# VectorE's path sums split around the sum of paths, the causal mask moved behind them

## The chip, the cores and the metric

One core of one Trainium2 chip runs the whole kernel. The metric is device time in microseconds (us) of one execution. Five engines work side by side, each in the order of its own program and tied to the others by semaphores: PE (TensorE, matmuls; its weight loads are listed as PEld), DVE (VectorE), ACT (ScalarE), POOL (GpSimd) and SP (SyncE, which here only issues DMAs).

## The reference

A decoder block over 32 sequences of 128 tokens, width 256, all in fp32:

```
x = layernorm(x + attn(x));  x = layernorm(x + cross_attention(ctx, x));  x = layernorm(x + moe(x))

attn: q, k, v = silu(conv4(x @ Wq | Wk | Wv));  beta = sigmoid(x @ Wb)
      delta = delta rule in chunks of 32 (a triangular inverse and a running state)
      paths = [fir3(v), fir15(v), fir64(v), delta, v]                 # 5 paths, 4 heads of 64
      stats = (mean, mean square, mean |.|, norm) of each path and head
      probs = softmax(gelu([x, stats] @ gW1 + gb1) @ gW2 + gb2, scaled) with a floor
      o = sum_p probs_p * paths_p;   out = (o * rsqrt(mean(o*o))) @ Wo
```

The change lies in the second half of attn: the solution of the delta rule, the statistics, the gate, the weighted sum of the paths, the output product and the first layernorm.

## The kernel before

The program runs stages one after the other: constants, projections, inverses and filters, `mix_paths`, then cross-attention, routing, experts and the final sum. Only `mix_paths` is touched. It handles the 32 sequences as 16 pairs. Every engine runs `staged_pair_loop(engine, 16, (step, lag), ...)`: in turn n each step of the list is done, in the order written, for pair n - lag. Several pairs are so in flight at once, and the written order of each list is the order in which that engine does its work. The semaphores say what a step must wait for; a step that waits holds up all that stands behind it on the same engine. Below, turn n is named after this count, and a turn is measured from one start of `shift_logits` on DVE (line L1104) to the next.

The lists are these, with the lag in brackets.

- DVE before: delta_sums (2), square_sums (2), mask_scores (1), sum_paths (3), mix_norm (3), path_sums (1), scale_mix (3), scale_delta (1), residual (3), shift_logits (2), ln_shift (3), probabilities (2).
- PE: scores (1), cross_blocks (1), then solve_rows(0) to (3) (1) alternating with hidden_x(0) to (3) (2), delta_rows (1), statsT (2), mixedT (3), hidden_stats (2), output (3), logits (2).
- ACT: square_delta (2), keep_cross (1), keep_rows(0) to (2) (1), square_mix (3), keep_rows(3) (1), square_paths (1), copy_stats (2), copy_mixed (3), gelu twice (2), exps (2), normalize (3).
- POOL: weight (3), norms (2), make_rhs (0), mix_inverse (3), ln_inverse (3).

The steps that matter here, with their lines: `mask_scores` (L1060) multiplies the scores of `scores` (L842), in PSUM, by the causal mask; `delta_rows` (L886) on PE multiplies the masked scores with the solution rows, and waits for `masked` and for the last `keep_rows` (L983). `path_sums` (L1083 on the three filtered paths, L1084 on the value) sums each path and its magnitude over each head, for both sequences t = 0 and 1 of the pair, eight reductions in all. `sum_paths` (L1140, L1145, L1148) adds the weighted paths and waits for POOL's `weight` (L1231). `mix_norm` (L1154, L1157) needs ACT's square (L1028); POOL's `mix_inverse` (L1239) takes the power -1/2; `scale_mix` (L1163) applies it; `mixedT` (L940) transposes the result for `output` (L948). `statsT` (L893) transposes the statistics of the pair before, `copy_stats` (L1001) moves them to SBUF, `hidden_stats` (L918) is the gate's first product with them, `gelu` (L1012), `logits` (L928), `shift_logits` and `probabilities` follow.

Of the kernel before, what the change touches and what calls it, by code (L numbers as in the profile page):

```python
# [75 lines left out]
def staged_pair_loop(eng, count, *stages):  # L76


    most = max(lag for _, lag in stages)
    fill = most + most % 2 + 2  # L80

    def turn(n):
        for step, lag in stages:
            if 0 <= n - lag < count:
                step((n - lag) // 2, (n - lag) % 2)

    for n in range(fill):
        turn(n)
    with eng.Fori(fill // 2, count // 2) as j:
        for u in range(2):  # L90
            for step, lag in stages:
                step(j + (u - lag) // 2, (u - lag) % 2)
    for n in range(count, count + most):
        turn(n)
# [28 lines left out]
def is_early(j, u, count):  # L123

    return isinstance(j, int) and 2 * j + u < count
# [25 lines left out]
def value_heads(M, n):  # L151

    return M.value[:, :, bass.ds(n, 1), :].rearrange("p (h k) b c -> p h k (b c)", k=HK)
# [7 lines left out]
def filtered_heads(M, n):  # L161

    return M.filtered[:, :, :, bass.ds(n, 1), :].rearrange("p f (h k) b c -> p (f h) k (b c)", k=HK)
# [536 lines left out]
def mix_paths(nc, M):  # L700
# [7 lines left out]
    P, W, PW = 2, DV * H, 2 * DV * H  # L708
    PAIRS = B // P
    with signals(nc) as signal, ExitStack() as ctx:  # L710
# [53 lines left out]
        statsT_mm = signal("statsT_mm")  # L764
# [32 lines left out]
        def tile(j, u, t):  # L797
            return P * (2 * j + u) + t
# [252 lines left out]
        def _(dve):  # L1051
# [20 lines left out]
                                  wide(M.rq[:, pairs(j, u), :].rearrange("p b h -> p (b h)"), [128, P * H, DV], 2),  # L1072
                                  ALU.mult).then_inc(delta_kept, 1)

            def path_sums(j, u):
                i = 2 * j + u
                if not is_early(j, u, 2):

                    dve.wait_ge(statsT_mm, i - 1)
                for t in range(P):  # L1080
                    fir, val = filtered_heads(M, tile(j, u, t)), value_heads(M, tile(j, u, t))
                    for s, mag in ((0, False), (2, True)):
                        dve.tensor_reduce(stat[:, u, t, 0:12, s], fir, AX.XY, ALU.add, apply_absolute_value=mag)  # L1083
                        dve.tensor_reduce(stat[:, u, t, 16:20, s], val, AX.XY, ALU.add, apply_absolute_value=mag)  # L1084

            def delta_sums(j, u):
                i = 2 * j + u
                dve.wait_ge(delta_kept, i + 1)
                for s, mag in ((0, False), (2, True)):
                    dve.tensor_reduce(stat[:, u, :, 12:16, s], delta[:, u, :, :].rearrange("p b (h d) -> p b h d", d=DV),  # L1090
                                      AX.X, ALU.add, apply_absolute_value=mag)
# [92 lines left out]
            def ln_shift(j, u):  # L1184
# [4 lines left out]
                dve.scalar_tensor_tensor(out=ln_s[:, :], in0=mv[:, :, 0], scalar=-1.0, in1=ln_r[:, :], op0=ALU.mult,  # L1189
                                         op1=ALU.mult).then_inc(shift_made, 1)  # L1190

            staged_pair_loop(dve, PAIRS, (delta_sums, 2), (square_sums, 2), (mask_scores, 1), (sum_paths, 3), (mix_norm, 3),
                             (path_sums, 1), (scale_mix, 3), (scale_delta, 1), (residual, 3), (shift_logits, 2), (ln_shift, 3),
                             (probabilities, 2))

        @block.gpsimd
        def _(pool):
# [1125 lines left out]
```

## Time and profile before

| | |
|---|---|
| time, three runs | median 2091.64 us (2087.59 to 2106.17) |
| the profiled execution | 2096.82 us, its span 2095.1 us |
| busy over the span | PE 1568.9 us (75%), PEld 1231.9 (59%), DVE 1011.6 (48%), ACT 634.0 (30%), POOL 647.8 (31%) |
| mean granted TensorE clock | 0.794 of full |

Times in the rows are us from the start of the span. The granted clock is a share of 2.4 GHz, so 1.00 is 2.4 GHz and 0.50 is 1.2 GHz. The mixing stage is one fifth to one quarter of the span, so what the change does there has to be read from this stage, not from the shares of the table.

### The profile page before, as it was taken

What the parts mean: (1) busy time and instruction counts of PE and PEld (TensorE: products, weight loads), DVE (VectorE), ACT (ScalarE), POOL (GpSimd) and SP (SyncE); (2) the same over time, 40 slices, a digit from 0 to 9 for tenths busy, and PEclk for the clock granted to TensorE, in tenths of its full rate; (3) what the DMA queues carried; (4) which work ended last, traced back from release to release, by engine and by line L of the source; (5) the groups of instructions that cost most, each with busy time, mean ns of one, the idle gap of its engine ahead of it and who ended that gap; (6) DMA issues with size and microseconds to landing.
All of it is one profiled execution on the core that took longest, in us unless ns stands there. A gap on an engine that the chain in (4) does not pass through costs nothing. (4 is left out here: it accounts for less than half of the span.)

```text
span 2095.1 us, 27839 instructions
## 1 busy us (share of the span) xinstructions
PE 1568.9 (75%) x8700; PEld 1231.9 (59%) x8701; DVE 1011.6 (48%) x1987; ACT 634.0 (30%) x1261; POOL 647.8 (31%) x481
## 2 busy tenths in 40 slices
PE   5786838957888888830788888888826899999861
PEld 2554537956666766620677777877413566666630
DVE  4565639915766666640565555555401122122155
ACT  3231306954444444420222222222200122222212
POOL 4645550004555455540211221122271000000066
PEclk9676755558888787865898888988867999999975
DMA  4425335434222222109310111000221012112134
GB/s 112 136 82 160 100 92 152 131 117 96 71 66 59 57 70 70 41 10 334 110 37 24 29 35 35 25 27 28 74 105 48 28 55 59 56 55 60 52 111 146
DMA packets 188436, 165.21 MB, mean 79 GB/s; under 512 B 70400, under 2 KB 160096, under 8 KB 187488
## 3 DMA queue, kind: packets, MB, share of 16 engines
q1 hardware_dynamic: 129024, 100.29, 17.7%
q10 hardware_dynamic: 53216, 47.49, 6.9%
q0 software_dynamic: 6144, 16.79, 2.6%
q8 instruction: 27, 0.44, 0.1%
q14 instruction: 25, 0.20, 0.0%
HBM read 98.45 MB, written 56.62 MB: 74 GB/s over the span
## 5 line engine op out<-in xcount | busy, mean ns | idle before, releaser
L2125 POOL DMA_INDIRECT gathered<-outs,row_of_token x64 | 62.4, 975 | 423.4 <-POOLq L139 404.9
L1383 PE MATMUL attend_psum<-ctxT_tile,w_src 128*128 128x128 f32 x512 | 91.4, 353 | 62.0 <-ACT x_tile L1483 62.0
L2067 DVE TENSOR_TENSOR hidden<-unit_psum,gate 128x352 f32<-128x352 f32 x72 | 37.8, 525 | 206.7 <-ACT gate L2042 206.7
L654 PE MATMUL fir_psum<-window,toep 96*96 96x128 f32 x512 | 116.7, 401 | 23.3 <-DMA toep<-in_fir 21.1
L654 PEld LDWEIGHTS fir_psum<-window,toep 96*96 96x96 f32 x512 | 111.7, 257 | 28.2 <-DMA window<-value 20.5
L667 ACT ACTIVATE filtered<-fir_psum 32x512 f32 (+1 forms) x192 | 112.9, 588 | 46.9 <-PE fir_psum L654 42.2
L1383 PEld LDWEIGHTS attend_psum<-ctxT_tile,w_src 128*128 128x128 f32 x512 | 87.2, 265 | 64.5 <-issue 63.2
L2022 PE MATMUL unit_psum<-wd,hiddenT 128*128 (+1 forms) x432 | 111.9, 395 | 10.6 <-issue 9.8
L346 PE MATMUL proj_psum<-xT_block,wqkv 128*128 128x512 f32 x192 | 97.7, 662 | 26.0 <-DMA xT_block<-in_xT 22.5
L1216 POOL TENSOR_TENSOR path_stats<-path_stats,plus_half 128x40 f32<-128x40 f32 x16 | 108.7, 6796 | 25.4 <-DVE path_stats L1097 25.4
L479 DVE SCALAR_TENSOR_TENSOR conv_acc<-proj_psum,conv_taps,conv_acc 128x508 f32<-128x508 f32 (+1 forms) x144 | 96.2, 735 | 38.3 <-ACT conv_acc L401 38.3
L1658 POOL TENSOR_TENSOR ln_stats<-ln_mean_var,minus_half 128x1 f32<-128x1 f32 x32 | 18.5, 577 | 287.8 <-DVE ln_mean_var L1620 287.8
L2005 PE MATMUL unit_psum<-wg,rowsT 128*128 x288 | 98.4, 465 | 0.6 <-ACT rowsT L2036 0.6
L2005 PE MATMUL unit_psum<-wu,rowsT 128*128 x288 | 98.2, 464 | 0.0
L2022 PEld LDWEIGHTS unit_psum<-wd,hiddenT 128*128 128x128 f32 (+1 forms) x432 | 76.4, 190 | 33.0 <-issue 25.2
L384 PE MATMUL proj_psum<-qkv_block 64*128 64x128 f32 x256 | 33.3, 438 | 74.6 <-DVE decay_gram L515 74.6
L1653 POOL TENSOR_TENSOR scores<-scores,score_max 128x1024 f32<-128x1024 f32 x32 | 60.7, 1897 | 88.4 <-DVE score_max L1595 88.4
L346 PEld LDWEIGHTS proj_psum<-xT_block,wqkv 128*128 128x128 f32 x192 | 39.2, 213 | 79.6 <-issue 69.3
L1699 PE MATMUL early_psum<-early_x2T,wg 128*128 128x512 f32 (+1 forms) x72 | 37.6, 648 | 53.2 <-DVE early_hiddenT L1716 46.9
L384 PEld LDWEIGHTS proj_psum<-qkv_block 64*128 64x128 f32 x256 | 28.6, 325 | 80.3 <-DVE decay_gram L515 77.7
L1936 POOL DMA_INDIRECT rows<-x,row_of_token x64 | 61.9, 967 | 39.4 <-DVE row_of_token L1881 20.1
L2005 PEld LDWEIGHTS unit_psum<-wu,rowsT 128*128 128x128 f32 x288 | 55.3, 192 | 31.1 <-issue 1.0
(267 smaller groups left out, 3692.0 us busy)
## 6 DMA issues: line engine op xcount, KB each, us to landing
gate_part<-in_gw1s SPq DMA_DIRECT2D x8, 1280.0 KB, 10.7
rows<-zero_row ACTq DMA_DIRECT2D x9, 1024.0 KB, 10.4
unit_rows<-rows SPq DMA_DIRECT2D x72, 128.0 KB, 2.3
outs<-unit_out ACTq DMA_DIRECT2D x72, 128.0 KB, 2.5
ndg<-decay_gram ACTq DMA_DIRECT2D x8, 1024.0 KB, 7.1
neg_decay_gram<-ndg SPq DMA_DIRECT2D x16, 512.0 KB, 4.5
ctxT_tile<-in_ctxT SPq DMA_DIRECT2D x32, 256.0 KB, 3.5
window<-value SPq DMA_DIRECT2D x32, 192.0 KB
```

Of the source, the lines that this page charges most:

```text
L346: mm = pe.matmul(psum[:, b, :], wqkv[:, m // KD, k, (m % KD) * 128:(m % KD) * 128 + 128], xT[:, u, k, :], start=(k == 0), stop=(k == KD - 1))
L384: mm = pe.matmul(psum[:, G_BANK + h % 2, at:at + L], kT, kT, start=True, stop=True)
L479: ins = dve.scalar_tensor_tensor(out=acc[:, :, s:L], in0=raw[:, :, 0:L - s], scalar=taps[:, m // KD, m % KD, TAPS - 1 - s:TAPS - s], in1=a ...
L654: mm = pe.matmul(psum[0:NFIR * QUART, u, TC * w + c, :], toep[:, w, :, :, c].rearrange("p f t -> p (f t)"), window[:, u, :, :, TC * w + c] ...
L667: act.activation(M.filtered[q * QUART:(q + 1) * QUART, f, bass.ds(n, 1), :, :].rearrange("p k b c -> p (k b) c"), psum[f * QUART:(f + 1) * ...
L1216: pool.tensor_tensor(stat[:, u, :, :, 3], stat[:, u, :, :, 1], wide(M.plus_half[:, 0:1].broadcast_to([128, NP * H]), [128, P, NP * H], 1), ...
L1383: pe.matmul(psum[:, u, FRONT, m * L:m * L + L], w_src[:, k, m * 128:m * 128 + 128], cT[:, u, k, :], start=(k == 0), stop=(k == NK - 1))
L1653: pool.tensor_tensor(sc[:, u, :, :], sc[:, u, :, :], wide(mx[:, u, :], [128, XH, L], 2), ALU.subtract).then_inc(shifted[u], 1)
L1936: pool.indirect_dma_start(out=M.rows_dram[:, :], out_offset=bass.IndirectOffsetOnAxis(ap=M.place[:, i, b:b + 1], axis=0), in_=M.x2[:, b, : ...
L2005: mm = pe.matmul(psum[:, u, bank, 0:EH], rowsT[:, u, k, :], w[:, bass.ds(chosen["gate_up"], 1), k, :].rearrange("p e n -> p (e n)"), start ...
L2022: mm = pe.matmul(psum[:, u, DOWN, 0:D], hidT[0:HR[t], u, t, :], M.wd[0:HR[t], bass.ds(chosen["down"], 1), t, :].rearrange("p e n -> p (e n)"),
L2125: pool.indirect_dma_start(out=got[:, b % NBUF, i, :], out_offset=None, in_=M.outs_dram[:, :], in_offset=bass.IndirectOffsetOnAxis(ap=M.pla ...
```

## The change

`path_sums` becomes `path_sums(t)`, a step for one sequence of the pair: four reductions instead of eight. The first stands in front of `sum_paths`, where `mask_scores` stood, and keeps the wait on `statsT_mm`; the second stands behind `mix_norm`; `mask_scores` follows it. No instruction is added or dropped. The lists of PE, ACT, POOL and SP are as they were.

```diff
-            def path_sums(j, u):
-                i = 2 * j + u
-                if not is_early(j, u, 2):
-                    dve.wait_ge(statsT_mm, i - 1)
-                for t in range(P):
+            def path_sums(t):
+                def step(j, u):
+                    i = 2 * j + u
+                    if t == 0 and not is_early(j, u, 2):
+                        dve.wait_ge(statsT_mm, i - 1)
                     fir, val = filtered_heads(M, tile(j, u, t)), value_heads(M, tile(j, u, t))
                     for s, mag in ((0, False), (2, True)):
                         dve.tensor_reduce(stat[:, u, t, 0:12, s], fir, AX.XY, ALU.add, apply_absolute_value=mag)
                         dve.tensor_reduce(stat[:, u, t, 16:20, s], val, AX.XY, ALU.add, apply_absolute_value=mag)
+                return step
...
-            staged_pair_loop(dve, PAIRS, (delta_sums, 2), (square_sums, 2), (mask_scores, 1), (sum_paths, 3), (mix_norm, 3),
-                             (path_sums, 1), (scale_mix, 3), (scale_delta, 1), (residual, 3), (shift_logits, 2), (ln_shift, 3),
-                             (probabilities, 2))
+            staged_pair_loop(dve, PAIRS, (delta_sums, 2), (square_sums, 2), (path_sums(0), 1), (sum_paths, 3), (mix_norm, 3),
+                             (path_sums(1), 1), (mask_scores, 1), (scale_mix, 3), (scale_delta, 1), (residual, 3), (shift_logits, 2),
+                             (ln_shift, 3), (probabilities, 2))
```

## Rows read from the trace of the kernel before

**Rows 1.** Windows view of the mixing stage: busy us of each engine, then the clock

```profile
core 0: us, PE busy (x) PEld busy (x) DVE busy (x) ACT busy (x) POOL busy (x), PEclk, DMA share, GB/s
460.00:935.00 475.00, 372.17 (x2648) 310.98 (x2648) 302.58 (x584) 206.74 (x366) 242.57 (x171) 0.78 0.24 60
```

**Rows 2.** Timeline, start of shift_logits in turns 2, 7 and 16

```profile
502.74 0.20 DVE L1104 TENSOR_TENSOR gate_logits<-mix_psum,gb 128x40 f32<-128x40 f32 x1 [6.21 <-PE mix_psum L928]
...
639.46 0.20 DVE L1104 TENSOR_TENSOR gate_logits<-mix_psum,gb 128x40 f32<-128x40 f32 x1
...
891.63 0.20 DVE L1104 TENSOR_TENSOR gate_logits<-mix_psum,gb 128x40 f32<-128x40 f32 x1
```

**Rows 3.** Timeline of turn 8, VectorE: start, duration, and idle time before in brackets

```profile
643.34 2.81 DVE L1097 TENSOR_REDUCE path_stats<-path_squares 128x40 f32<-128x2560 f32 x1
...
646.07 1.21 DVE L1060 TENSOR_TENSOR causal_scores<-mix_psum,causal 128x1024 f32<-128x1024 f32 x1
...
647.37 1.96 DVE L1140 TENSOR_REDUCE mixed<-filtered 128x256 f32 x2
...
652.50 0.95 DVE L1083 TENSOR_REDUCE path_stats<-filtered 128x12 f32 x1
...
654.88 0.94 DVE L1083 TENSOR_REDUCE path_stats<-filtered 128x12 f32 x1
...
657.25 0.68 DVE L1163 TENSOR_TENSOR mixed<-mixed,mixed_inverse_norms 128x512 f32<-128x512 f32 x1
...
665.03 0.69 DVE L1169 TENSOR_TENSOR residual<-mix_psum,x_tiles 128x512 f32<-128x512 f32 x1 [6.49 <-PE mix_psum L948]
...
666.90 0.19 DVE L1104 TENSOR_TENSOR gate_logits<-mix_psum,gb 128x40 f32<-128x40 f32 x1
```

**Rows 4.** Timeline of turn 8, the other engines

```profile
646.50 0.61 POOL L1231 TENSOR_TENSOR value<-value,gate_exps 128x256 f32 x1
...
649.23 1.13 PE L907 MATMUL mix_psum<-xT_tiles,gate_w_x 128*128 128x256 f32 x4
...
651.64 0.59 ACT L983 ACTIVATE beta_r_v_to_solution<-mix_psum 32x512 f32<-32x512 f32 x1
...
652.28 2.51 PEld L886 LDWEIGHTS mix_psum<-beta_r_v_to_solution,causal_scores 128*128 128x128 f32 x16 [2.33 <-ACT beta_r_v_to_solution L983]
...
654.56 0.40 PEld L893 LDWEIGHTS mix_psum<-ident,path_stats 128*80 128x80 f32 x2
...
654.94 1.63 POOL L1239 TENSOR_TENSOR mixed_inverse_norms<-mixed_mean_squares,minus_half 128x8 f32<-128x8 f32 x1
...
655.52 0.38 ACT L1001 ACTIVATE path_statsT<-mix_psum 80x256 f32<-80x256 f32 x1 [1.17 <-PE mix_psum L893]
...
658.06 0.71 PEld L940 LDWEIGHTS mix_psum<-ident,mixed 128*128 128x128 f32 x4 [3.10 <-issue]
...
658.76 3.11 PEld L918 LDWEIGHTS mix_psum<-path_statsT,gw1s 80*128 80x128 f32 x8
...
664.52 1.97 PEld L928 LDWEIGHTS mix_psum<-gw,gate_hiddenT 128*128 128x128 f32 x16
```

**Rows 5.** Windows view of turn 8, PE alone: us, busy, granted clock, DMA

```profile
639.50:650.40 10.90, 10.60 (x110) 1.00 0.08 24
650.40:652.30 1.90, 0.01 (x1) 1.00 0.93 287
652.30:655.40 3.10, 3.10 (x18) 0.68 0.95 223
655.40:658.10 2.70, 0.04 (x2) 0.50 0.59 124
658.10:663.60 5.50, 5.50 (x15) 0.50 0.00 0
663.60:667.00 3.40, 3.40 (x30) 1.00 0.01 1
```

**Rows 6.** Timeline of turn 10, then a windows row of its tail, PE alone

```profile
713.49 3.11 PEld L918 LDWEIGHTS mix_psum<-path_statsT,gw1s 80*128 80x128 f32 x8
...
720.10 3.75 PEld L928 LDWEIGHTS mix_psum<-gw,gate_hiddenT 128*128 128x128 f32 x16
...
724.00 0.20 DVE L1104 TENSOR_TENSOR gate_logits<-mix_psum,gb 128x40 f32<-128x40 f32 x1 [1.17 <-PE mix_psum L928]
...
713.50:724.00 10.50, 10.50 (x36) 0.50 0.08 25
```

**Rows 7.** Waits between 500 and 860 us: total, times, longest

```profile
PE mix_psum L940 <- DVE mixed L1163: 38.4, 13, 3.5
DVE mixed_mean_squares L1154 <- ACT residual L1028: 9.4, 13, 0.8
DVE mixed L1140 <- POOL value L1231: 3.1, 9, 0.4
```

## The prediction

> **What bounds the kernel now.** The change stays inside the mixing stage, so I read that first: between 460 and 935 us no engine is busy all the time (PE 372 of 475 us, DVE 303, POOL 243) [rows 1]. The stage is a loop of waits, and its length is set by the loop that closes last. The starts of shift_logits give the beat: turn 2 at 502.74, turn 16 at 891.63 [rows 2], 388.89 us for 14 turns, 27.78 us each. I then followed one turn, turn 8, from 639.46 to 666.90 (27.44 us) [rows 2, 3], and asked at each step what ended last. I count from 639.46 as zero.
>
> DVE works almost without a break from 0 to the end of scale_mix: square_sums gives way to mask_scores at 6.61, sum_paths starts at 7.91, mix_norm gives way to path_sums at 13.04, scale_mix starts at 17.79 and ends at 18.47 [rows 3]. Its waits on the way are small: in 13 turns 3.1 us for POOL's weighting and 9.4 us for ACT's square [rows 7]. PE then waits for scale_mix (38.4 us in those 13 turns [rows 7]) and does mixedT at 18.60, hidden_stats at 19.30 and logits at 25.06; shift_logits follows at 27.44 [rows 3, 4]. DVE itself is idle for 6.49 us of that time, ahead of the residual [rows 3]. So the loop is DVE for two thirds and PE for one third. The important thing is what PE does in the meantime: delta_rows starts at 12.82, statsT at 15.10, both done before scale_mix [rows 4]. They are off the path, under DVE's path sums.
>
> **The change part by part.** DVE's work from 0 to scale_mix is the same set of instructions in another order. *First half of path_sums ahead of sum_paths:* from 652.50 to the third L1083 at 654.88 it takes 2.38 us [rows 3], so sum_paths starts at 6.61 + 2.38 = 8.99 instead of 7.91. POOL's last weighting ends at 647.11, which is 7.65 [rows 4], so that wait goes: 3.1 us in 13 turns, 0.24 a turn. *sum_paths and mix_norm* take the 5.13 us that lie between 647.37 and 652.50 [rows 3], ACT's square included, and end at 14.12. ACT's list puts square_mix ahead of the last keep_rows, so keep_rows, now at 12.18 [rows 4], slides to about 13.2, which will not matter. *Second half:* 2.38 us, to 16.50. *mask_scores:* 646.07 to its end 1.21 us later, and about 1.20 to what follows [rows 3], to 17.70. *scale_mix* starts there, against 17.79 now. POOL's mix_inverse ends at 656.57, which is 17.11 [rows 4]; it stands behind norms and make_rhs on POOL and begins no later than now, so it does not decide. DVE's part of the loop is worth 0.1 us less a turn, 1 us in all.
>
> *mask_scores behind everything:* here is the price. delta_rows needs the mask, and behind delta_rows on PE stand statsT, mixedT, hidden_stats, output and logits. PE runs dry when hidden_x(3) ends, 10.9 after zero [rows 4, 5]; today it resumes at 12.82 and is ready again before scale_mix. After the change it resumes at 17.75, and delta_rows and statsT, until now hidden, lie on the path between the mask and mixedT. Only 0.7 us of that is covered by scale_mix, which runs meanwhile. scores, the solver's matmuls and the DMA loads behind solve_rows keep their places, and scale_delta, which waits for delta_rows on DVE, falls to about 21.5 with only the residual (now at 25.57 [rows 3]) behind it: nothing there.
>
> The length of delta_rows depends on the clock. In turn 8 the granted clock was 1.00 up to 652.3 and fell to 0.50, that is 1.2 GHz, while delta_rows ran (mean 0.68), after PE had been without work for 1.9 us; it stayed there through the second pause of 2.7 us, until 663.6, 5.5 us after PE had resumed [rows 5]. After the change PE is without work from 10.9 to 17.75, 6.85 us in one piece, longer than both pauses of today together (4.6), so I take the clock as already low when delta_rows starts. At the high level, or nearly, delta_rows takes 2.28 us from its first load to that of statsT [rows 4]. For the low level no row of delta_rows exists; the nearest is logits of turn 10, also 16 loads of 128x128 with small products: 3.90 us from first load to shift_logits [rows 6], against 2.38 in turn 8 [rows 3, 4]. The ratio puts delta_rows at 2.28 * 3.90 / 2.38 = 3.7. I take 3.6; the bounds are 2.3 and 3.9.
>
> statsT to hidden_stats: ACT's copy must come between. It ended at 655.90, 1.34 us after statsT's first load [rows 4], so hidden_stats starts at 17.75 + 3.6 + 1.35 = 22.7, against 19.30 now: +3.4. The tail from there to shift_logits was 8.14 us in turn 8, of which the clock was low for 4.84 [rows 3 to 5], and 10.51 in turn 10, with the clock at 0.50 all along [rows 6]. If 4.84 of 10.51 us of low work were done in turn 8, the other 54% took 3.30, so a tail wholly at 2.4 GHz is about 6.1 (an estimate). Now the clock has had 5 us of matmuls ahead of hidden_stats rather than 0.7. If it rises 5.5 us after PE resumes, as in turn 8, that is 0.5 us into the tail, the tail is 6.3 (each low us costs 1 - 6.1 / 10.51 = 0.42); if only hidden_stats brings it back, as now, 8.14. delta_rows are short products, so I lean to the latter and take 7.6. The turn becomes 22.7 + 7.6 = 30.3 us, against a mean of 27.78: +2.5.
>
> How many turns: the steps of lag 1 and lag 3 meet in turns 3 to 16, 14 turns. In turns 1 and 2 the mask waits for scores or has nothing of lag 3 beside it, and in turn 17 no mask is left; I cost these at nothing. 14 * 2.5 = 35 us. The profiled execution took 2096.8 us (span 2095.1), which would become 2132; the median of the runs shown lies 5.2 us below it, so 2091.6 + 35 = 2127, 1.7% slower.
>
> The Trainium skill, page "TensorE: Matmul & The Clock Gate", section "HAM oscillation — how this bites in real kernels", says that a burst of matmuls behind a pause starts at the lower clock, and that a loop with such a pause pays for it every time; it speaks against gathering PE's idle time into one pause. The trace agrees: mixedT and hidden_stats, behind the pause of 2.7 us, ran at 0.50 [rows 5]. By that rule delta_rows cost the 3.6 us of the sum; without it they would cost 2.3, and the sum would be 14 * 1.3 = 18 us less, 2109.
>
> **The rivals.** *The clock comes back at once.* Same path, but the rise comes while delta_rows run. The turn is 17.75 + 2.3 to 3.6 + 1.35 + 6.1, 27.5 to 28.8, so between nothing and +14 us in all, about 2092 to 2106. For it: PE is continuously at work from 17.75 on. Against: turn 10, busy all along and still low after 10.5 us [rows 6].
>
> *The clock comes back late.* Turn 10's tail of 10.51 in many turns: 22.7 + 10.5 = 33.2, up to +5.4 a turn; if in half of the turns, 2127 + 7 * 2.9 = 2147, in all 2168. For it: turns at the rate of turn 10 exist today. Against: they are few.
>
> *The other side: the clock never falls.* With its work in one piece PE might keep 2.4 GHz through the turn. The turn is then 17.75 + 2.28 + 1.34 + 6.1 = 27.47, 0.3 us less than the mean of 27.78 (which holds slow turns such as turn 10), -4 us in all: 2087, not slower. It decides if the low stretch of today hangs on the broken work from 652.3 to 658.1 rather than on the pause. Against: the clock fell in turn 8 while the pauses were only 1.9 and 2.7 us [rows 5], and the new one is 6.85.
>
> *The mask does not decide.* If delta_rows had slack to give, only the saved waits would count, -1 to -3 us, 2090. It would need the mask by 19.30 - 1.34 - 2.28 = 15.7, so that hidden_stats could start as now; it comes at 17.7, two microseconds late even at the high clock.
>
> **How the numbers follow.** My forecast (mask on the path, delta_rows low, tail 6.3 to 8.2, so 2108 to 2138): 0.73. Clock back at once: 0.09. Late: 0.12. Never falls: 0.02. Mask not deciding: 0.02. Something else: 0.02. Range 2106 to 2150: it leaves out the last three cases, the early one and half or less of the late, 0.2 in all. A measurement of this kernel tells about 1% from no change, so slower begins at 2112.6: the upper nine tenths of the forecast, the late case and a bit more, 0.80; within 1%: 0.18; faster: 0.02.
>
> **What the profile after would show.** The mask (L1060) starts about 16.5 us after shift_logits, and delta_rows directly behind it, with PE or PEld idle for some 6.8 us on DVE's causal_scores; the wait of mixedT on scale_mix gone; sum_paths no longer waiting for POOL; scale_mix still at 17.7; the granted clock 0.50 over all of delta_rows; hidden_stats at 22.7; the beat of L1104 about 30.3 us. The forecast is wrong if delta_rows start before the mask's end would allow, if they take under 2.5 us, or if the rise of the clock moves ahead of hidden_stats.

## The result, and the profile after

The changed kernel takes 2127.39 us (median of four runs, 2126.91 to 2146.53) against 2094.43 us of the kernel before beside it: 1.0174 times, 95% interval 1.010 to 1.0248. A second series (below) gave 1.0224, interval 1.0184 to 1.0265. So it is slower by about 2%: both intervals lie above 1, and the two medians are 1.7 and 2.2% up. Its profiled execution took 2126.91 us, span 2125.2 us, 30.1 us more than the profiled execution of before. From here on a turn is counted as ahead of the prediction, the beat is the mean length of a turn, and a mean is that of turns 3 to 16.

Lines of the source move: below `path_sums` all of them lie two further down, inside it one. Timeline of the changed kernel, turn 7; the rows answer to those of turn 8 before [rows 2 to 4]:

```profile
627.05 0.19 DVE L1106 TENSOR_TENSOR gate_logits<-mix_psum,gb 128x40 f32<-128x40 f32 x1
...
633.28 0.94 DVE L1084 TENSOR_REDUCE path_stats<-filtered 128x12 f32 x1
...
635.65 1.94 DVE L1142 TENSOR_REDUCE mixed<-filtered 128x256 f32 x2
...
640.68 0.95 DVE L1084 TENSOR_REDUCE path_stats<-filtered 128x12 f32 x1
...
642.52 1.63 POOL L1241 TENSOR_TENSOR mixed_inverse_norms<-mixed_mean_squares,minus_half 128x8 f32<-128x8 f32 x1
...
643.06 1.22 DVE L1060 TENSOR_TENSOR causal_scores<-mix_psum,causal 128x1024 f32<-128x1024 f32 x1
644.19 0.69 DVE L1165 TENSOR_TENSOR mixed<-mixed,mixed_inverse_norms 128x512 f32<-128x512 f32 x1
644.39 3.49 PEld L886 LDWEIGHTS mix_psum<-beta_r_v_to_solution,causal_scores 128*128 128x128 f32 x16 [6.85 <-issue]
644.42 3.65 PE L886 MATMUL mix_psum<-beta_r_v_to_solution,causal_scores 128*128 128x64 f32 x16 [6.48 <-DVE causal_scores L1060]
647.65 0.40 PEld L893 LDWEIGHTS mix_psum<-ident,path_stats 128*80 128x80 f32 x2
...
648.96 3.08 PEld L918 LDWEIGHTS mix_psum<-path_statsT,gw1s 80*128 80x128 f32 x8
...
655.43 1.97 PEld L928 LDWEIGHTS mix_psum<-gw,gate_hiddenT 128*128 128x128 f32 x16
...
657.81 0.20 DVE L1106 TENSOR_TENSOR gate_logits<-mix_psum,gb 128x40 f32<-128x40 f32 x1
```

From 627.05 as zero: the mask starts at 16.01 (before, in turn 8: 6.61), and delta_rows start at 17.34, 0.11 us behind the mask's end (before: 12.82). PE had nothing to do for 6.48 us, and the bracket names who ended that: DVE's causal_scores. scale_mix starts at 17.14, a little sooner than before. But it no longer decides anything: delta_rows run for 3.26 us, statsT after them, and hidden_stats come at 21.91 instead of 19.30. The turn is 30.76 us.

Windows view of the same turn, PE alone (us, busy, granted clock, DMA share, GB/s), beside [rows 5]:

```profile
633.40:637.90 4.50, 4.50 (x42) 1.00 0.00 0
637.90:644.40 6.50, 0.05 (x1) 0.79 0.91 221
644.40:655.30 10.90, 10.88 (x37) 0.50 0.05 14
655.30:657.80 2.50, 2.50 (x25) 1.00 0.00 0
```

The clock fell in the pause, and stayed at 1.2 GHz for 10.9 us of unbroken work. In turn 8 before, it rose 5.5 us after PE had resumed from its second pause [rows 5]. Waits between 530 and 900 us, which answer to [rows 7]:

```profile
PE mix_psum L886 <- DVE causal_scores L1060: 79.3, 12, 6.9
...
ACT path_statsT L1001 <- PE mix_psum L893: 72.3, 12, 6.1
...
DVE mixed_mean_squares L1156 <- ACT residual L1028: 8.7, 12, 0.8
```

The wait of mixedT on scale_mix and that of sum_paths on POOL have left the list; the new head among PE's waits is the mask, 6.6 us in each of twelve turns. The beat, by the starts of shift_logits in turns 2 and 16:

```profile
504.32 0.20 DVE L1106 TENSOR_TENSOR gate_logits<-mix_psum,gb 128x40 f32<-128x40 f32 x1 [6.05 <-PE mix_psum L928]
...
933.54 0.20 DVE L1106 TENSOR_TENSOR gate_logits<-mix_psum,gb 128x40 f32<-128x40 f32 x1
```

429.22 us for 14 turns, 30.66 each, against 27.78 [rows 2]: 40.3 us more. That is 10 us more than the growth of the whole span. The windows view by stage says where they went; first the kernel before, its attention stage, then the changed kernel, its mixing and its attention stage (busy us of PE, PEld, DVE, ACT, POOL, then the clock):

```profile
944.00:1482.00 538.00, 412.18 (x2880) 365.55 (x2880) 275.76 (x642) 109.13 (x224) 100.46 (x96) 0.83 0.22 67
```

```profile
451.30:985.30 534.00, 388.06 (x2656) 329.78 (x2656) 304.65 (x592) 207.77 (x368) 247.21 (x178) 0.76 0.23 56
986.20:1511.00 524.80, 405.58 (x2880) 359.50 (x2880) 275.72 (x642) 109.06 (x224) 100.34 (x97) 0.84 0.23 69
```

The mixing stage took 534.0 us against 493.2 (449.8 to 943.0), 40.8 more; the attention stage behind it, the same code, took 13.2 less.

### The profile page after: what moved, and what is told of

It is laid out like the page before. It is cut to its first block and busy times, and to the rows that moved or that the text cites. A ratio compares the mean times of both kernels' runs of the same rounds, so it can differ in the third digit from the quotient of the medians.

```text
span 2125.2 us, 27839 instructions
## 1 busy us (share of the span) xinstructions
PE 1569.9 (74%) x8700; PEld 1237.6 (58%) x8701; DVE 1015.6 (48%) x1987; ACT 633.5 (30%) x1261; POOL 647.2 (30%) x481
## 5 line engine op out<-in xcount | busy, mean ns | idle before, releaser
L886 PE MATMUL mix_psum<-beta_r_v_to_solution,causal_scores 128*128 128x64 f32 x256 | 54.4, 401 | 90.7 <-DVE causal_scores L1060 90.0
L886 PEld LDWEIGHTS mix_psum<-beta_r_v_to_solution,causal_scores 128*128 128x128 f32 x256 | 52.0, 310 | 96.1 <-issue 95.2
L1660 POOL TENSOR_TENSOR ln_stats<-ln_mean_var,minus_half 128x1 f32<-128x1 f32 x32 | 18.4, 575 | 274.2 <-DVE ln_mean_var L1622 274.2
```

What stands on the lines that cost most here:

```text
L886: mm = pe.matmul(psum[:, DELTA, at:at + DV], att[:, t, h, :], xs[:, u, at:at + DV], start=True, stop=True)
```

## The experiments

All ten start from one of the two kernels. "Stage" is the mixing stage, from the first to the last instruction of `mix_paths`. Of the engines' lists the diffs show only the steps that move and their neighbours. The ratio is to the kernel before on the same chip, with its 95% interval.

| run | beat, us | delta_rows from | hidden_stats from | tail | stage, us | ratio of times |
|---|---|---|---|---|---|---|
| before | 27.78 | 12.64 | 19.09 | 8.69 | 493.2 | 1 |
| changed | 30.66 | 17.43 | 21.99 | 8.67 | 534.0 | 1.0174 (1.010 to 1.0248) |
| e1, split, mask in front | 27.23 | 14.63 | 19.03 | 8.19 | 486.3 | 0.9947 (0.9917 to 0.9977) |
| e2, mask alone moved | 31.62 | 18.96 | 23.56 | 8.05 | 547.8 | 1.0295 (1.026 to 1.0329) |
| e3, mask in the middle | 28.43 | 15.09 | 19.33 | 9.10 | 502.5 | 1.0035 (1.0012 to 1.0059) |
| e4, changed, fill too long | 28.66 | 20.13 | 22.96 | 5.70 | 506.0 | 1.0071 (1.0045 to 1.0098) |
| e5, before, pauses filled | 24.78 | 12.84 | 18.94 | 5.84 | 450.8 | 0.9831 (0.9765 to 0.9897) |
| e6, changed, pause filled | 26.06 | 17.63 | 20.36 | 5.70 | 470.0 | 0.9913 (0.9885 to 0.9941) |
| e7, gate ahead of mixedT | 26.67 | 12.68 | 15.50 | 11.17 | 479.3 | 0.9917 (0.9889 to 0.9945) |
| e8, e7 and a fill | 24.37 | 13.01 | 15.79 | 8.58 | 445.5 | 0.9807 (0.9752 to 0.9861) |
| e9, changed once more | 30.66 | 17.43 | 21.99 | 8.68 | 533.6 | 1.0224 (1.0184 to 1.0265) |
| e10, e8 and a second fill | 23.92 | 12.74 | 15.53 | 8.39 | 440.4 | 0.9771 (0.9725 to 0.9818) |

Columns three and four count from shift_logits of the turn before; the tail is from hidden_stats to the next shift_logits (in e7, e8 and e10 mixedT and scale_mix lie in between).

**Order: e2, e1, e3.** e2 is the kernel before with one step moved:

```diff
-(mask_scores, 1), (sum_paths, 3), (mix_norm, 3), (path_sums, 1), (scale_mix, 3)
+(sum_paths, 3), (mix_norm, 3), (path_sums, 1), (mask_scores, 1), (scale_mix, 3)
```

> The kernel before with path_sums whole and in its place, and mask_scores alone moved behind it. Theory: this one edit brings the whole cost. sum_paths starts as early as POOL's weighting allows (7.7), mix_norm ends at about 12.5, the mask starts at about 16.1 to 16.5, delta_rows at about 17.4, the beat is 30.3 to 31 us and the mixing stage 529 to 539 us, as in the changed kernel. Rival (the split costs): beat and stage close to before, below 29 and 510 us.

The move alone costs more than the whole change: beat 31.62, stage 547.8 us, beyond the 529 to 539 expected. The timeline of its turn 8 (which begins at 661.68) shows the miss:

```profile
669.60 1.96 DVE L1140 TENSOR_REDUCE mixed<-filtered 128x256 f32 x2 [1.23 <-POOL value L1231]
...
679.47 1.22 DVE L1060 TENSOR_TENSOR causal_scores<-mix_psum,causal 128x1024 f32<-128x1024 f32 x1
680.61 0.68 DVE L1163 TENSOR_TENSOR mixed<-mixed,mixed_inverse_norms 128x512 f32<-128x512 f32 x1
680.81 3.49 PEld L886 LDWEIGHTS mix_psum<-beta_r_v_to_solution,causal_scores 128*128 128x128 f32 x16 [8.64 <-issue]
```

sum_paths cannot start before POOL has weighted the paths. In the kernel before the mask filled that time; in the changed kernel the first half of the path sums fills it; here nothing does, DVE waits 1.23 us, and the mask starts at 17.79 instead of 16.1. So the late mask is the cost, and the split wins a part of it back: 31.62 - 30.66 = 0.96 us a turn. In the means the mask and hidden_stats come 1.53 and 1.57 us later than in the changed kernel; 0.62 us of that is hidden by a shorter tail, because in six of e2's turns the clock came back sooner (below).

e1 takes the other half of the change:

```diff
-(path_sums(0), 1), (sum_paths, 3), (mix_norm, 3), (path_sums(1), 1), (mask_scores, 1), (scale_mix, 3)
+(mask_scores, 1), (path_sums(0), 1), (sum_paths, 3), (mix_norm, 3), (path_sums(1), 1), (scale_mix, 3)
```

> The changed kernel with mask_scores put back in front of the first half of path_sums; the split stays. Theory (the late mask puts delta_rows and statsT on the path): all of the cost goes. The mask starts 6.2 to 6.6 us after shift_logits, delta_rows at about 12.8 as before, and the beat falls from 30.7 us to that of before, 27.8; sum_paths starts at about 10.2, so that scale_mix comes no sooner than 17.8. The mixing stage, 493 us before and 534 after, is within 5 us of 493. Rival (the split costs: half of the path sums ahead of sum_paths delays the square and the norm): delta_rows are early, but scale_mix comes later than 18.5 and the beat stays above 28.5, the stage above 503.

The cost is gone, and the kernel is a little faster than before. Timeline of its turn 8 (from 639.48):

```profile
653.16 0.63 ACT L1028 ACTIVATE residual<-mixed 128x512 f32<-128x512 f32 x1 [5.30 <-DVE mixed L1150]
653.81 0.59 ACT L983 ACTIVATE beta_r_v_to_solution<-mix_psum 32x512 f32<-32x512 f32 x1
...
654.45 3.48 PEld L886 LDWEIGHTS mix_psum<-beta_r_v_to_solution,causal_scores 128*128 128x128 f32 x16 [4.49 <-ACT beta_r_v_to_solution L983]
...
657.31 0.68 DVE L1165 TENSOR_TENSOR mixed<-mixed,mixed_inverse_norms 128x512 f32<-128x512 f32 x1
657.71 0.40 PEld L893 LDWEIGHTS mix_psum<-ident,path_stats 128*80 128x80 f32 x2
```

One detail was expected wrongly: delta_rows do not start at 12.8 but at 14.63 in the mean. sum_paths is 2 us later, ACT's square of the mix with it, and the last keep_rows stands behind that square on ACT; delta_rows wait for keep_rows. In the mean that delay costs nothing: hidden_stats come at 19.03 against 19.09. But the slack is used up. In turn 8 statsT starts at 18.23 and is done at 19.1, behind the end of scale_mix at 18.5 (in turn 8 before it was done at 15.9), and hidden_stats come at 19.63, 0.33 us later than in turn 8 before. The 0.55 us a turn that e1 wins over the kernel before lie in the tail, 8.19 against 8.69. The mean clock from turn 3 to 16 is 0.82 here and 0.80 before; why it is higher was not tried.

e3 puts the mask in the middle, ahead of the second half:

```diff
-(mix_norm, 3), (path_sums(1), 1), (mask_scores, 1), (scale_mix, 3)
+(mix_norm, 3), (mask_scores, 1), (path_sums(1), 1), (scale_mix, 3)
```

> The changed kernel with mask_scores between mix_norm and the second half of path_sums. Theory: the mask is done at about 14.8 us after shift_logits, delta_rows run from 14.9 to between 17.0 and 18.2, statsT after them, so mixedT and hidden_stats come 0 to 1 us later than before: the beat is 27.5 to 28.8 us, the mixing stage 489 to 510 us. Rival (any delay of the mask is paid in full): 2 us more a turn than before, the beat about 29.8, the stage about 521.

delta_rows at 15.09, hidden_stats 0.24 us later than before, beat 28.43 (0.65 more), stage 502.5: as expected, with the longest tail of the three (9.10). The first 2.45 us of delay of delta_rows cost 0.24 us at hidden_stats; the next 2.34 us, from e3 to the changed kernel, cost 2.66. The edge lies where delta_rows and statsT stop fitting ahead of scale_mix, and so it depends on the clock: in the four turns of e3 whose delta_rows ran at the high level (1.73 us to the load of statsT) hidden_stats came at 18.4 to 18.8, in the eight with 3.26 us at 19.4 to 20.1.

**Clock: e4, e6, e5.** These fill PE's pauses with matmuls whose result nothing reads; all else is done as in the reference. Each fill waits for the residual of the pair before, so that DVE has read the bank that it writes to.

```diff
+            def keep_busy(count):
+                def step(j, u):
+                    pe.wait_ge(residual_kept, 2 * j + u)
+                    for _ in range(count):
+                        pe.matmul(psum[:, TAIL, 0:256], gw1x[:, 0, 0:128], gw1x[:, 0, 0:256], start=True, stop=True)
+                return step
...
-                             (delta_rows, 1), (statsT, 2), (mixedT, 3), ...
+                             (keep_busy(22), 3), (delta_rows, 1), (statsT, 2), (mixedT, 3), ...
```

> The changed kernel, and in the pause of PE between hidden_x(3) and delta_rows 22 matmuls of 128x256 on a constant tile are done into the bank of the tail, about 6.2 us, whose result nothing reads. They add no result and change none. Theory with the clock as a part of its own (the pause of 6.4 us lowers the clock, and delta_rows, hidden_stats and output then run at 1.2 GHz): granted clock near 1.00 through the turn, delta_rows 2.0 us instead of 3.3, the tail from hidden_stats to shift_logits 6.1 to 6.6 instead of 9.0, the beat 26.8 to 27.8 instead of 30.7, the mixing stage 480 to 495 us. Rival (the clock is no cause, what counts is the order alone): beat and stage as in the changed kernel, 30 to 31 and 534 us. If the fill overruns the pause the beat is up to 0.5 us longer than the theory says.

The fill was sized wrongly, at 6.2 us; it took 9.66. PE's rows of turn 8, and the windows row of all fourteen turns (us, busy, clock):

```profile
660.28 9.66 PE L957 MATMUL mix_psum<-gate_w_x 128*128 128x256 f32 x44
```

```profile
505.40:906.60 401.20, 397.87 (x2941) 1.00 0.25 61
```

The 22 matmuls of the program stand as 44 in the trace: in fp32 each is recorded twice. I had taken the price of one, 0.28 us, from hidden_x's rows (four in 1.13 us), which are two matmuls of the program. The true price is 9.66 / 22 = 0.44 us (6.64 / 15 in e6 gives the same), not the 0.41 of the expectation of e5. delta_rows so started at 20.13, 2.7 us later than in the changed kernel, and still the beat was 2.0 us shorter: delta_rows took 1.83 us and the tail 5.70. The clock is a part of its own; the rival, that the order alone counts, fell.

e6 has 15 in place of 22. e5 is the kernel before with 4 ahead of delta_rows and 8 ahead of mixedT.

> The changed kernel, with 15 idle matmuls in the pause ahead of delta_rows, 6.2 us, so that they no longer overrun it. Beside the kernel before with its own fill this gives the price of the order alone, at one clock. Theory: delta_rows at about 17.3 to 17.5 after shift_logits, for 1.84 us, hidden_stats at 20.2, tail 5.7, the beat 25.9 to 26.1: 1.1 us more a turn than the kernel before with its fill, 15 us in all, so that of the 2.9 us a turn that the change costs about 1.1 is order and 1.8 is clock. Rival (the order is all of it, the clock costs both kernels the same): 2.9 us a turn more than the kernel before with its fill, a beat of about 27.8.

> The kernel before, with 4 of the same idle matmuls (0.41 us each, as measured in the fill before this one) between hidden_x(3) and delta_rows and 8 between statsT and mixedT, sized to the two pauses of PE. Their result is read by nothing. Theory (in both kernels the low clock is a price of its own): clock near 1.00 through the turn, mixedT at about 18.3 as now, the tail from hidden_stats to shift_logits 5.7 us instead of 8.7, the beat 24.8 to 25.3 instead of 27.8, the mixing stage about 455 us instead of 493, the total 2050 to 2060. Rival (the tail is held by ACT's copy, table load and gelus, not by the clock): tail and beat fall by less than 1 us.

e6, PE and DVE in turn 8 (from 634.20), and its windows row over the turns:

```profile
644.93 6.64 PE L957 MATMUL mix_psum<-gate_w_x 128*128 128x256 f32 x30
652.01 1.97 PE L886 MATMUL mix_psum<-beta_r_v_to_solution,causal_scores 128*128 128x64 f32 x16 [0.44 <-DVE causal_scores L1069]
...
660.48 0.19 DVE L1115 TENSOR_TENSOR gate_logits<-mix_psum,gb 128x40 f32<-128x40 f32 x1
```

```profile
504.30:869.10 364.80, 359.66 (x2745) 0.99 0.27 67
```

The same two of e5, in its turn 8 (from 628.74):

```profile
641.56 2.00 PE L886 MATMUL mix_psum<-beta_r_v_to_solution,causal_scores 128*128 128x64 f32 x16 [0.19 <-ACT beta_r_v_to_solution L992]
...
653.49 0.20 DVE L1113 TENSOR_TENSOR gate_logits<-mix_psum,gb 128x40 f32<-128x40 f32 x1
```

```profile
503.80:850.70 346.90, 343.88 (x2661) 0.99 0.29 70
```

Both keep the clock at 0.99, and in both the fill starts delta_rows 0.20 us later than without it. At one clock the change costs 26.06 - 24.78 = 1.28 us a turn, 18 us in fourteen: delta_rows (1.8 us) and statsT on the path, less what scale_mix and mixedT took before. With the clock free it costs 2.88. The other 1.60 us a turn, 22 us, is what the one long pause adds in slow work: the low clock costs the kernel before 3.0 us a turn (27.78 - 24.78) and the changed one 4.6 (30.66 - 26.06). The expectation had 1.1 and 1.8.

**The same kernel again: e9.**

> The changed kernel unaltered, beside the kernel before on the same chip. In its first profile the mixing stage had grown by 40.8 us but the whole by 30.1, because the attention stage behind it, the same code, took 524.8 instead of 538.0 us. Theory (the attention stage differs from one execution to the next by 10 to 20 us, with its granted clock, whatever stands ahead of it): mixing stage 531 to 537 us again, attention anywhere between 524 and 547, ratio of the times 1.013 to 1.022. Rival (the later entry gives 13 us back in attention each time): attention at 525 again and the ratio at 1.013 to 1.017.

Mixing stage 533.6 us and the same beat to a hundredth. Attention took 538.6 us, and the ratio was 1.0224. So the 13 us that attention gave back in the first profile belong to that execution, not to the change: over all profiles this stage, whose code is the same in each, took between 524.8 us (the first of the changed kernel, and e1) and 546.4 us (e5), with a granted clock of 0.84 and 0.81. What sets it in one execution stays open.

**A version that beats both: e7, e8, e10.** The runs point to PE's pauses, so e7 fills the second one with useful work:

```diff
 PE:  -(statsT, 2), (mixedT, 3), (hidden_stats, 2), (output, 3), (logits, 2)
      +(statsT, 2), (hidden_stats, 2), (mixedT, 3), (output, 3), (logits, 2)
 ACT: -(copy_mixed, 3), (gelu(0), 2), (gelu(1), 2), (exps, 2), (normalize, 3)
      +(gelu(0), 2), (gelu(1), 2), (copy_mixed, 3), (exps, 2), (normalize, 3)
```

> The kernel before, with the gate's hidden_stats put ahead of mixedT on PE and the two gelus ahead of copy_mixed on ACT; all work is as in the reference. It puts useful work into the pause while DVE is not done. Theory: hidden_stats start at about 16.0 after shift_logits instead of 19.1 and run, at the low clock, until about 19.3; mixedT follows, output at about 20.8, logits at about 23.4; the beat 25.5 to 26.5 instead of 27.8, the mixing stage about 465 to 475 us. Rival (mixedT comes late by what hidden_stats now lasts ahead of it, and gains nothing): the beat within 0.5 us of 27.8.

hidden_stats run early, at 15.50, and in two microseconds, at the high clock and not at the low one as expected; but the beat fell only to 26.67 and the stage to 479.3 us, short of the 25.5 to 26.5 and 465 to 475 expected. In turns 6 to 13 the clock fell at about 18.4, and output and logits ran at 1.2 GHz; turns 3 and 16, in which it did not fall, took 23.3 us. e8 adds `keep_busy(4)` ahead of delta_rows, e10 also `keep_busy(3)` between hidden_stats and mixedT.

> The same order, with 4 idle matmuls in the pause between hidden_x(3) and delta_rows. Theory: the clock stays at 1.00, hidden_stats run from 16.0 to 17.6, mixedT at 18.3 right behind scale_mix, output at 19.8, logits at 21.5, the beat 23.6 to 24.2, the mixing stage about 440 us, the total 2035 to 2045. Rival (the clock falls all the same, from the pauses that are left): beat and stage as without the fill.

> The gate-first order with its 4 idle matmuls ahead of delta_rows, and 3 more (1.2 us) in the pause that is left between hidden_stats and mixedT. Theory: in the run without them three of fourteen turns still lost the clock and took 27.3 us; now the clock stays at 1.00, all turns take 23.3 to 23.9, the mixing stage 436 to 442 us instead of 445.5, the total 2040 to 2052. Rival (the clock falls from the wait of output on ACT, 1.2 us, not from this pause): two to four slow turns again, stage 445.

e8 reached 24.37 us, a stage of 445.5 and a median of 2054.66, each a little above what was expected; turns 6 and 15 still took 27.3 (the expectation of e10 says three turns; it is two). In e10 all turns from 4 to 16 took 23.7 to 24.0, which speaks for the pause between hidden_stats and mixedT as what had still let the clock fall. Windows row of its turns:

```profile
504.90:839.80 334.90, 314.02 (x2523) 0.99 0.30 73
```

Its beat is 23.92 us and its median 2044.79 us, 0.9771 of the kernel before (interval 0.9725 to 0.9818), 4% under the changed kernel. It is the best of all, though 7 of the matmuls of every turn do nothing but keep the clock.

## Why the prediction came out

The forecast was 2127 us, 2106 to 2150, and the median 2127.39. Point by point, measured as means of turns 3 to 16:

| step | forecast | measured |
|---|---|---|
| sum_paths starts | 8.99 | 8.71 |
| mask starts | 16.5 | 16.10 |
| delta_rows start, length | 17.75, 3.6 | 17.43, 3.2 |
| scale_mix starts | 17.7 | 17.27 |
| hidden_stats start | 22.7 | 21.99 |
| tail | 7.6 (6.3 to 8.14) | 8.67 |
| beat | 30.3 | 30.66 |
| 14 turns against before | +35 | +40.3 |
| profiled execution | +35 | +30.1, then +39.3 in the repeat |

**The path was right.** The mask ended last, delta_rows and statsT lay bare behind it, and DVE's own chain, to scale_mix, got shorter by 0.4 us in the mean (17.63 to 17.27). e2 shows the mask as the cause by itself, e1 shows that without it nothing is lost, and e3 places the point at which it starts to cost: I had it at a mask done by 15.7, and e3's, done at about 15.0, costs 0.24 us at hidden_stats. The 15.7 held delta_rows at their high-clock length of 2.28; at the 3.26 us of most turns of e3 the same sum, 19.30 - 1.34 - 3.26, gives 14.7.

**The hit on the number is better than the sum.** Two errors and a chance cancel, and that the median came within 1 us of the forecast is luck. The DVE steps were read from turn 8, whose square_sums end 0.3 us later than in the mean, so the mask came 0.4 us sooner than forecast; delta_rows took 0.4 us less. Against that the tail was mis-sized by 1.1 us: I let the clock come back 0.5 to 4.9 us into it because PE would have worked for 5 us ahead of hidden_stats. In turn 7 it came back 10.9 us after PE resumed, not 5.5; only two turns, 8 and 14, were near the forecast (7.0 us, and a turn of 29.3). The work that PE now does first, delta_rows, did not bring the clock back sooner. My estimate of 6.1 for a tail wholly at 2.4 GHz erred the other way: it is 5.70 in e6 and 5.84 in e5. What sets the moment at which the clock rises is not shown. It is not the order of the work alone, for behind the same order it varied: in the kernel before from 5.5 us after PE resumed (turn 8) to 15.8 (turn 10, first row), in e2 from 6.9 (turn 11, second row) to 12.3 (turn 13, third row):

```profile
712.70:728.50 15.80, 15.70 (x68) 0.50 0.06 17
...
776.40:783.30 6.90, 6.84 (x27) 0.50 0.00 0
...
839.40:851.70 12.30, 12.30 (x43) 0.50 0.00 0
```

The stage so cost 40.8 us instead of 35, and the first profile gave 11 of these back in stages that the change does not touch. The stage's 40.8 us on the 2091.6 of the forecast make 2132 us, 2.0%; the two series lie on both sides of it, at 1.7 and 2.2% (2138 us). All are inside the range. The forecast's own band was summed a little wide: its longest tail, 8.2, gives 14 * 3.1 = 44 us and 2135, not 2138.

**The split.** The sum gave it 0.24 us a turn, the wait on POOL that was left with the mask as its cover. e2 shows its real worth with the mask late: 1.53 us at the mask, 0.96 a turn. Take the mask away from that place and 1.23 us of wait are open unless something else fills them. I priced the edits one by one against the kernel before, where each cover was still in place.

**The rivals.** The clock back at once: in no turn. Back late: 12 of 14 turns had a tail above 8.14, but the longest turn took 31.5 us, not 33.2. The clock never falling: only when PE was given work (e6), and then the changed order is indeed faster than the kernel before, 0.9913, though slower than the kernel before with its own fill (e5); the 27.47 us that the prediction gave that turn were 26.06. The mask not deciding: refuted by the wait of 6.6 us on it.

The Trainium skill, page "TensorE: Matmul & The Clock Gate", section "HAM oscillation — how this bites in real kernels", describes a loop in which a wait of a few microseconds sends TensorE back to the lower clock, so that the burst behind each wait starts slow. The runs agree: the pause of 6.5 us is followed by 10.9 us at 0.50, and filling it takes 4.6 us off a turn in the mean. The pause of 2.7 us, which the prediction named in support, is no proof of it: the clock had been low since delta_rows, ahead of that pause [rows 5].

## What to carry to other kernels

When a step moves in one engine's order, look for what another engine does behind it in its own order: the mask itself is 1.2 us, the matmuls and the transposition that queue behind it were hidden and are now bare. Price a move with the covers as they will be, not as they are: the gap that the moved step filled is open again. And treat a pause of TensorE as two costs, the wait and the slow work after it; here the second was the larger (1.60 of 2.88 us a turn). Twelve useless matmuls a turn (e5), or seven with a step pulled forward (e10), took 42 and 53 us off the stage, more than the 41 that the change added; the step alone (e7) took 14.

## What the runs showed of the hardware that was not expected

- After the pause of 6.5 us the clock stayed at 1.2 GHz through 10.9 us of gapless work (delta_rows first), after the one of 2.7 us through 5.5 us (mixedT and hidden_stats first). Behind one and the same order it varied by a factor of nearly two in e2 (6.9 to 12.3 us) and nearly three in the kernel before (5.5 to 15.8); the cause stays open.
- With 22, 15 or 12 idle matmuls a turn the granted clock over fourteen turns was 1.00, 0.99 and 0.99; delta_rows took 1.83 us (e4) against 3.26 at 0.50.
- A matmul of the program in fp32 stands twice in the trace: 22 as 44, 15 as 30; one of 128x256 took 0.44 us at 2.4 GHz, back to back.
- One stage with the same code took 524.8 to 546.4 us from one execution to another, a difference of 4%, with DVE, ACT and POOL busy for the same time to 0.3 us and PE's mean clock between 0.84 and 0.81.
